# Normalization order, filler matmuls, V's bias and weight loads in the front of a fused attention and expert layer

## The reference, cut to what matters

```python
xn = _layernorm(x, axis=-1)
x = x + attn(xn) + ffn(xn)
# attn
q, k, v = proj(Wq, bq), proj(Wk, bk), proj(Wv, bv)
q, k = _apply_rope(q, sin, cos), _apply_rope(k, sin, cos)
attn = softmax(where(cam, q @ k.T * scale, neg))
out = (attn @ v) @ Wo.T + bo
# ffn
logits = xn @ router_w.T
top_vals, top_idx = top_k(logits, 2)
expert, weight = top_idx[:, 0], softmax(top_vals)[:, 0]
out = (silu(xn @ gate_w.T) * (xn @ up_w.T)) @ down_w.T   # of the row's expert
out = out * weight
```

## Time and profile before

| what | us |
|---|---|
| median of 3 runs | 379.81 |
| lowest and highest of them | 377.82, 380.61 |
| the profiled execution's own time | 378.44 |
| its span | 376.6 |
| TensorE busy | 360.9 |
| VectorE busy | 331.0 |
| ScalarE busy | 265.3 |
| GpSimd busy | 72.0 |

### The profile page before, as it was taken

One profiled execution on the slowest core, in us unless ns is written; L12 is line 12 of the kernel. 1 busy time (PEld: TensorE's weight loads), 2 busy tenths in 40 slices (PEclk: granted clock), 3 DMA queues, 4 the chain that ended last, 5 costly groups with the idle time before them and its releaser, 6 DMA issues.

```text
span 376.6 us, 12257 instructions
## 1 busy us (share of the span) xinstructions
PE 360.9 (96%) x4670; PEld 204.4 (54%) x4670; DVE 331.0 (88%) x684; ACT 265.3 (70%) x538; POOL 72.0 (19%) x87
## 2 busy tenths in 40 slices
PE   0899999999999999999999999999999999999996
PEld 0665467675664554555645555455455554643364
DVE  5779789997767999999999999999999999998655
ACT  1533567664445888888888888888888888899920
POOL 5001744553000020120210202121222020210002
PEclk9999999999999999999999999999999999999999
DMA  7999646765511212132232221232213222111116
GB/s 234 404 382 261 152 132 184 220 192 169 143 51 44 61 33 60 50 83 62 49 76 60 74 62 45 76 81 68 74 45 85 68 57 74 34 35 29 46 29 224
DMA packets 30794, 40.58 MB, mean 108 GB/s; under 512 B 10772, under 2 KB 25876, under 8 KB 30160
## 3 DMA queue, kind: packets, MB, share of 16 engines
q1 hardware_dynamic: 28680, 34.62, 30.8%
q0 software_dynamic: 1872, 5.11, 5.5%
q10 hardware_dynamic: 192, 0.13, 0.1%
HBM read 25.78 MB, written 11.70 MB: 100 GB/s over the span
## 4 chain that ended last, share of the span: by engine, by line
PE 92%; ACT 2%; DMA 2%; SPq 1%; issue 1%; DVE 1%; ACTq 0%; DVEq 0%
PE ps L791 22%; PE ps L821 21%; PE ps L716 14%; PE ps L667 7%; PE ps L729 6%; PE ps L594 5%; PE ps L680 5%; PE ps L799 3%; PE ps L705 2%; DMA bqk<-bqk_in 2%; PE ps L583 1%; PE ps L692 1%; PE ps L653 1%; PE ps L576 1%; PE ps L570 1%
## 5 line engine op out<-in xcount | busy, mean ns | idle before, releaser
L1125 DVE TENSOR_REDUCE mx<-ps 128x1 f32<-128x512 f32 x232 | 150.2, 683 | 3.7 <-PE ps L716 0.9
L1426 ACT ACTIVATE probs<-ps 128x512 f32<-128x512 f32 x192 | 101.8, 599 | 18.4 <-PE ps L821 17.4
L821 PE MATMUL ps<-q_op,k_op 98*32 98x512 bf16 (+1 forms) x1104 | 112.2, 381 | 0.2
L716 PE MATMUL ps<-k_op,q_op 96*32 96x512 bf16 x672 | 76.1, 381 | 0.0
L1128 DVE TENSOR_REDUCE mx_tail<-ps 128x2 f32<-128x410 f32 x116 | 66.8, 576 | 3.7 <-PE ps L729 3.5
L821 PEld LDWEIGHTS ps<-q_op,k_op 98*32 98x32 bf16 (+1 forms) x1104 | 39.3, 96 | 33.7 <-ACT wqk L1426 5.2
L791 PE MATMUL ps<-probs,v_op 128*32 128x512 f32 x384 | 52.5, 592 | 0.0
L502 POOL COPY v_op<-v_all 128x192 f32<-128x192 f32 x16 | 7.0, 443 | 187.5 <-PE ps L791 187.5
L1426 ACT ACTIVATE dn<-ps 77x512 f32<-77x512 f32 x64 | 34.2, 591 | 8.3 <-PE ps L821 8.2
L496 POOL DMA_INDIRECT o_st<-sorted_rows,token_of x23 | 28.2, 1228 | 57.0 <-DVE token_of L1054 29.2
L716 PEld LDWEIGHTS ps<-k_op,q_op 96*32 96x32 bf16 x672 | 25.1, 96 | 22.0 <-DVE mx L1125 9.6
(11 more groups left out here) (142 smaller groups left out, 490.1 us busy)
## 6 DMA issues: line engine op xcount, KB each, us to landing
q_parts<-parts SPq DMA_DIRECT2D x12, 256.0 KB, 2.8
sorted_results<-ys SPq DMA_DIRECT2D x23, 128.0 KB, 2.4
gu<-gu_in SPq DMA_DIRECT2D x1, 2816.0 KB, 11.5
q_op<-q_parts SPq DMA_DIRECT2D x11, 192.0 KB, 3.4
tab<-tab_in SPq DMA_DIRECT2D x1, 2048.0 KB, 11.3
sorted_rows<-xn SPq DMA_DIRECT2D x4, 512.0 KB, 5.9
xnT<-o_st SPq DMA_DIRECT2D x62, 32.0 KB, 2.3
tab<-softmax_recips SPq DMA_DIRECT2D x15, 128.0 KB
```

The lines of the kernel that those rows point to most:

```text
L716: ins = pe.matmul(bank(t % 2)[r:r + CW, :], q_op[slot][0:KR, P * t + r:P * t + r + CW], k_op[slot][0:KR, 0:NWIDE], start=True, stop=True)
L821: ins = pe.matmul(bank(4 + u % RING)[r:r + w, :], k_op[h % OPS][:, c0 + r:c0 + r + w], q_op[h % OPS][:, QB * b:QB * b + QB], start=True, s ...
L1125: dve.tensor_reduce(mx[:, slot, t:t + 1], bank(t % 2)[:, 0:NWIDE], AX.X, ALU.max).then_inc(wide_reduced, 1)
L1426: act.activation(prob[c][0:rows, QB * b:QB * b + QB], bank(4 + u % RING)[0:rows, :], ACT.Exp, scale=SCALE).then_inc(exp_done, 1)
```

## The change

- **Front, VectorE.** `moments` is split into `statistics` and `moments`. The order is now statistics, aggregates and normalization of a group, then the next group; the statistics of tiles 12 and 13 stand before the third normalization. The addition of the constant is gone: ScalarE's root takes it as its bias from a tile `eps`. The last group is normalized like the others, two tiles on each engine. VectorE copies the pair 6 to `xnT`, ScalarE the pair 7.
- **Front, ScalarE.** `root(g)` stands directly before the normalization of its own group, or a little before it. The bias of the first key half stands before the third normalization. ScalarE's queue issues the load of the identity matrix.
- **Front, TensorE.** VectorE writes zeros to a part of `q_op1`, and `keep_running` multiplies them, 512 columns at a time: 16 times at the start, and 6, 2, 2 and 2 times between the pairs. All logits are made in one group of eight matmuls. Two chunks of V stand before pairs 6 and 7, and half of projection 2 before the sums of the slots.
- **GpSimd** writes the ones of `v_all` first and those of the three `k_op` after the logits.
- **V's bias.** `add_bv` is gone. ScalarE copies V's chunks in its place (`copy_v`). Before head 0 TensorE multiplies bv, spread over the partitions, with wo, and VectorE adds the result to the output's bias, which is what GpSimd adds to x.
- **Loads.** x comes without other transfers between its groups. Keys' and queries' weights come separately, the tables in three parts. The middle part of the tables and `dn` are issued after a wait for the fourth gather, ahead of the remaining key parts; `wo` is issued at step 6.

The diff, cut:

```diff
@@ sync
-                if g == 1:
-                    sp.dma_start(const[:], const_d).then_inc(const_in, 16)
-                    sp.dma_start(rt[:], rt_d).then_inc(rt_in, 16)
...
+            load_tab(1)
             store_part(0, 0)
+            sp.wait_ge(xs_in[3], 16)
+            load_tab(2)
             sp.dma_start(dn[0:80, :], dn_d[0:80, :]).then_inc(down_in, 16)
             sp.dma_start(dn[80:IH, :], dn_d[80:IH, :]).then_inc(down_in, 16)
-            sp.wait_ge(xs_in[1], 16)
-            sp.dma_start(wo[:], wo_d).then_inc(wo_in, 16)
...
+                if s == 6:
+                    sp.dma_start(wo[:], wo_d).then_inc(wo_in, 16)
@@ tensor
+            def keep_running(times):
+                for _ in range(times):
+                    pe.matmul(bank(6), q_op[1][:, 0:P], q_op[1][:, 0:QB], start=True, stop=True)
+            pe.wait_ge(warm_ready, 1)
+            keep_running(16)
+            pe.wait_ge(ident_in, 16)
+            for pair in (0, 1):
+                turn_pair(pair)
+            keep_running(6)
+            for pair in (2, 3):
+                turn_pair(pair)
+            keep_running(2)
+            pe.wait_ge(wk_in, 16)
+            pe.wait_ge(xnT_ready, 1)
+            project(0)
...
+            project_v(V_ORDER[5])
+            pe.wait_ge(wq_in, 16)
+            project(2, (0,))
             pe.wait_ge(slot_ready, 1)
...
+            pe.wait_ge(wo_in, 16)
+            pe.wait_ge(bvo_in, 32)
+            for m in range(HC):
+                ins = pe.matmul(bank(3)[:, 0:HID], bv_col[:, m:m + 1].broadcast_to([P, P]),
+                                wo[:, HID * m:HID * m + HID], start=m == 0, stop=m == HC - 1)
+            ins.then_inc(bias_in_psum, 1)
             head_step(0, 0, first=True)
@@ vector
-                settle()
-                dve.tensor_scalar(var[:, 4 * g:4 * g + 4], mv[:, 4 * g:4 * g + 4, 1], EPS, None,
-                                  ALU.add).then_inc(var_ready, 1)
...
-            for g in range(1, 4):
-                moments(g)
-                normalize(g - 1)
+            statistics(0, 4)
+            moments(0)
+            normalize(0)
+            statistics(4, 8)
+            moments(1)
+            normalize(1)
+            statistics(8, 12)
+            moments(2)
+            statistics(12, 14)
+            normalize(2)
+            statistics(14, 16)
+            moments(3)
             normalize(3)
...
-            for n in range(NCH):
-                add_bv(n)
...
+            dve.wait_ge(bias_in_psum, 1)
+            dve.wait_ge(bvo_in, 32)
+            dve.tensor_tensor(bias, bank(3)[:, 0:HID], bias, ALU.add).then_inc(bias_ready, 1)
             head_step(0, 0, early=True)
@@ scalar
+            def copy_v(n):
+                c = V_ORDER[n]
+                rows = CHUNKS[c][1]
+                act.wait_ge(v_in_psum, n // 2 * 2 + 2)
+                act.copy(v_view[0:rows, :, c, 0:DH], v_bank(c).rearrange("p (h d) -> p h d", h=HEADS)
+                         ).then_inc(v_read, 1)
```

More of the change, by code:

```diff
@@ L115, in layer @@
         bvo = sb("bvo", [P, 2 * HID])
+        bias = bvo[:, HID:2 * HID]
+        bv_col = bvo[:, 0:HC]
         const = sb("const", [P, C_END])
@@ L211, in layer @@
         x_first = sem("x_first")
-        const_in, wqk_in, tab_in = sem("const_in"), sem("wqk_in"), sem("tab_in")
+        const_in, wk_in = sem("const_in"), sem("wk_in")
+        tab_in = [sem(f"tab_in{n}") for n in range(3)]
         wv_in, rt_in, gate_up_in, down_in, wo_in = (
             sem(n) for n in ("wv_in", "rt_in", "gate_up_in", "down_in", "wo_in"))
+        ident_in, wq_in, bqk_in, bvo_in = (sem(n) for n in ("ident_in", "wq_in", "bqk_in", "bvo_in"))
+        warm_ready = sem("warm_ready")
         dve_step = sem("dve_step")
@@ L479, in _ @@
         def _(pool):
-            for n in range(RING):
-                pool.memset(k_op[n][KR:KM, :], 1.0).then_inc(ones_ready, 1)
-                pool.wait_ge(ones_ready, n + 1)
+            pool.memset(v_all[:], 1.0).then_inc(ones_ready, 1)
+            pool.wait_ge(ones_ready, 1)
             pool.iota(lane, [[1, P]], base=0, channel_multiplier=0).then_inc(iota_ready, 1)
@@ L488, in _ @@
             pool.wait_ge(iota_ready, 3)
-            pool.memset(v_all[:], 1.0).then_inc(ones_ready, 1)
-            pool.wait_ge(ones_ready, RING + 1)
+            pool.wait_ge(logits_T_ready, 1)
+            for n in range(RING):
+                pool.memset(k_op[n][KR:KM, :], 1.0).then_inc(ones_ready, 1)
+                pool.wait_ge(ones_ready, n + 2)
             def gather(t):
@@ L533, in add_bias @@
             def add_bias(t):
-                pool.tensor_tensor(x_sb[:, t, :], x_sb[:, t, :], bvo[:, HID:2 * HID], ALU.add
+                if t == 0:
+                    pool.wait_ge(bias_ready, 1)
+                pool.tensor_tensor(x_sb[:, t, :], x_sb[:, t, :], bias, ALU.add
                                    ).then_inc(residual_ready, 1)
@@ L563, in turn_pair @@
                     pe.wait_ge(xnT_ready, pair - 3)
-                if pair % 2 == 0 or pair == NT // 2 - 1:
+                if pair % 2 == 0:
                     pe.wait_ge(xn_ready, pair // 2 + 1)
@@ L625, in _ @@
             ins.then_inc(logits_ready, 1)
-            for c in V_ORDER[2:4]:
+            for c in V_ORDER[3:5]:
                 project_v(c)
@@ L643, in _ @@
             ins.then_inc(slots_summed, 1)
-            for u in (2, 3):
-                project(u)
+            project(2, (1,))
+            project(3)
             def turn_rows(t):
@@ L897, in settle, with statistics @@
                 dve.wait_ge(dve_step, steps[0])
-            def moments(g):
-                for t in range(4 * g, 4 * g + 4):
+            def statistics(first, last):
+                for t in range(first, last):
                     if t == 0:
@@ L919, in normalize @@
                                          rstd[:, 4 * g:4 * g + 4], ALU.mult, ALU.mult).then_inc(scale_ready, 1)
-                for t in range(4 * g, 4 * g + (2 if g < 3 else 4)):
+                for t in range(4 * g, 4 * g + 2):
                     ins = dve.tensor_scalar(xn[:, t, :], x_sb[:, t, :], mv[:, t, 0:1], rstd[:, t:t + 1],
@@ L939, in _ @@
                                    0.0, None, ALU.is_gt))
+            dve.wait_ge(xT_in_psum, NT // 2 - 1)
+            dve.tensor_copy(xnT[:, :, S - 4 * P:S - 2 * P], bank(2).rearrange("p (m n) -> p m n", m=HC)
+                            ).then_inc(last_xnT_ready, 1)
             step(dve.tensor_scalar(same_token[:].rearrange("p (t e) -> p t e", t=NT),
@@ L1322, in biased @@
                                bias=bqk[:, col:col + 1], scale=1.0).then_inc(proj_read, 1)
+            act.dma_start(const[:, 0:C_TRI], const_d[:, 0:C_TRI]).then_inc(ident_in, 16)
             root(0)
-            for g in range(1, 4):
-                root(g)
-                normalize(g - 1)
-                copy_xT(2 * g - 2)
-                copy_xT(2 * g - 1)
-            copy_xT(6)
-            act.wait_ge(wqk_in, 32)
-            for odd in range(2):
-                biased(0, odd)
+            normalize(0)
+            copy_xT(0)
+            copy_xT(1)
+            root(1)
+            normalize(1)
+            copy_xT(2)
+            copy_xT(3)
+            root(2)
+            act.wait_ge(bqk_in, 16)
+            biased(0, 0)
+            normalize(2)
+            copy_xT(4)
+            root(3)
+            copy_xT(5)
+            normalize(3)
+            biased(0, 1)
+            copy_xT(7)
+            v_view = v_all[:].rearrange("p (h c w) -> p h c w", h=HEADS, c=NCH)
+            def copy_v(n):
[4 more added lines that the diff above has]
+                         ).then_inc(v_read, 1)
+            act.wait_ge(ones_ready, 1)
+            for n in (0, 1):
+                copy_v(n)
             act.wait_ge(logits_T_ready, 1)
@@ L1395, in _ @@
             highest(0)
+            for n in (2, 3):
+                copy_v(n)
             for odd in range(2):
                 biased(1, odd)
+            for n in (4, 5):
+                copy_v(n)
+            biased(2, 0)
             act.wait_ge(gap_ready, 1)
             act.activation(tk["ratio"][:], tk["gap"][:], ACT.Exp).then_inc(ratio_ready, 1)
-            for odd in range(2):
-                biased(2, odd)
+            biased(2, 1)
+            biased(3, 0)
             middle(0)
-            for odd in range(2):
-                biased(3, odd)
+            biased(3, 1)
             copy_rows(0)
```

87 lines of the change are left out of this document (40 added, 47 removed).

## The result

The changed kernel takes 385.57 us (median of 4 executions, 385.36 to 387.09) beside 379.96 for the kernel before, measured with it: ratio 1.0161, 95% interval 1.0124 to 1.0198. (The ratios in this document come with the measurements and are not quite the quotients of the medians, here 1.0148.) It is slower by 1.5 to 1.6%, where the forecast was 379.7 with a range up to 382.0. The profiled execution took 385.44 around a span of 383.5, which is 6.9 above the span of before (376.6).

The account below looks back on a forecast made before the run. TensorE, busy 96% of the span and carrying the chain of waits, was taken as the bound. Terms -0.8 + 0.7 = -0.1 on the median 379.81 gave 379.7 us; own range 378.5 to 380.7, eight in ten 375.6 to 382.0.

Parts of the forecast that it names:

- Part 1, the front: Reordered opening up to the first turn of gathered rows: TensorE gets there at 36.0 against 41.53, 5.5 us won if kept.
- rival C: Front zeros fail, TensorE stays at 1.2 GHz until 17, tokens no earlier than 34.8: +3.6, 383.4 us, chance 0.05.
- The stall of 0.8 us: VectorE's small operations in the opening: GpSimd lockout could return 0.8 us on the next one; none was counted.
- Part 2, the landing of the down weights: Down weights behind the fourth gather and tables' middle land at 51.6; TensorE stops 3.8 us before the first down product.
- rival B: TensorE's clock falls in the stop at the first down product: +1.0, with the bias +1.7, 381.5 us; chance 0.18.
- The cast: ScalarE's cast for projection 2 waits for stores behind the down weights until 52.4; VectorE's subtraction then wins nothing.
- Part 3, V's bias: Bias matmuls and VectorE's addition before head 0 delay its maxima: cost 0.4 to 1.2 us, taken as +0.7.
- TensorE's wait of 0.38: Before head 0, TensorE waited 0.38 us for ScalarE's last copy; the bias matmuls stand there, a maximum tile partly filling it.
- what part 1 leaves behind part 2: Front's gain remaining after the late down weights: taken as -0.8 us, bounds -5.5 to +1.
- rival A: Down weights load at 386 GB/s, not 217, and land at 48.7, nearly in time: -3.0, 376.8 us; chance 0.27.

Follow-up runs that it names:

- e6: Kernel before, with the down weights issued behind the fourth gather instead of behind the gate and up weights: 382.81 us, ratio 1.0092.
- e12: Changed kernel, with the stores of the other five key parts held back until the down weights have landed: 388.29 us, ratio 1.0232.
- e7: Changed kernel, with the first key group's two small parts stored ahead of SyncE's wait for the fourth gather: 385.47 us, ratio 1.0153.
- e1: Changed kernel without SyncE's wait for the fourth gather, order of transfers kept: 384.17 us, ratio 1.0153.
- e2: Changed kernel, wait kept, with the down weights issued ahead of the tables' middle: 384.05 us, ratio 1.0146.
- e4: Changed kernel, with V's bias added by VectorE as before and no product of bv and wo: 383.47 us, ratio 1.0115.
- e5: Changed kernel, down weights directly behind gate/up, then two small key parts, only the tables' middle behind the fourth gather: 378.62 us, ratio 0.998.
- e8: e5 with V's bias added on VectorE as before, without the bias product: 377.89 us, ratio 0.9949.
- e9: Changed kernel with the edits of e3 and e7 together: 383.56 us, ratio 1.0093.
- e3: Changed kernel, with 32 more zero matmuls on TensorE ahead of the wait for the down weights: 386.36 us, ratio 1.0207.
- e10: e8 with eight zero products ahead of the first turn of gathered rows: 377.61 us, ratio 0.9943.
- e11: e10 without the 28 zero products of the front: 378.08 us, ratio 0.9954.

## Why the prediction was wrong

**Part 1, the front, held.** First turned pair 7.77 (forecast 7.0), last copy of xnT ends at 18.8 (18.1), token numbers 31.66 (31.1), first turn of gathered rows 36.67 (36.0). The 0.7 us that is missing arises at the very start: the second half of the first group of x came 0.48 later than VectorE wanted it, and the small operations behind took the rest. The transposes run at full rate; rival C is out. The stall of 0.8 us that the prediction priced did not come back: VectorE's small operations in the first group took 0.38 (four aggregates), 0.18 and 0.16.

**Part 2, the landing of the down weights, is the step that failed.** The forecast put it at 51.6, with a stop of 3.8 us. It landed at 56.4, with a stop of 7.9. The 4.8 us between come from three terms:

- The wait ended at 40.66 instead of 40.1: +0.6.
- SyncE needs 0.57 and 0.60 us to issue the tables and the first part of the weights, so the last part is issued at 41.91. I had counted its issue at the wait's end: +1.25.
- The last part then took 14.47 us instead of 2.2 + 2.7 + 6.6 = 11.5: +3.0. In e6, with no tables ahead, it took 11.87, so the tables are worth about 2.6, as forecast (2.7), and the weights 11.87 - 2.2 = 9.7 instead of 6.6, or 149 GB/s and not 217.

Why 9.7 shows in the packet records of the traces, in which the weights have 88 packets of 16 KB. From the start of the first to the end of the last it takes 7.9 us in the kernel before (30.80 to 38.71), 9.1 in the changed kernel, 10.1 in e6 and 9.4 in e12. So the forecast was short by two things. First, I had read the rate in a stretch in the middle of the load: the same load took 7.9 us even in the trace of before, because its last eight packets need 1.7 us. Second, what else the DMA engines did in that time. The queue of GpSimd's gathers in it (packets, MB, share of 16 engines), in the order before (30.8 to 38.7), changed (46.1 to 55.2), e6 (42.8 to 53.0), e12 (47.0 to 56.4):

```profile
q0 software_dynamic: 41, 0.12, 7.8%
q0 software_dynamic: 135, 0.39, 23.8%
q0 software_dynamic: 110, 0.32, 25.2%
q0 software_dynamic: 139, 0.39, 25.4%
```

Before, the load ran nearly alone; behind the fourth gather it meets the gathers of the expert steps, and they take a quarter of the engines. The prediction says that gathers beside the load add, and adds nothing. By these shares they take 1.6 us (changed), 2.0 (e6) and 1.8 (e12) more of all 16 engines than before, and the load takes 1.2, 2.2 and 1.5 longer than before. So the sizes agree, but no run kept the gathers away from the load.

**The clock was rival B, and belonged in the sum.** I gave it 0.18 and 1 us. It fell in the stops of 7.9 us and more of the changed kernel, e7 and e12, and in those of e1, e2, e4, e5, e6 and e8, which were 1.9 to 5.7 us long. The Trainium skill, page "TensorE: Matmul & The Clock Gate", Part 1, was cited for it in the prediction; the trace agrees with it, and the 0.96 and 0.50 of the windows are the row. I had weighed the rule and left it out of the sum, and it was one side of the tie that e9 measured at 2.0 to 2.6 us.

**The cast.** The forecast had it start at 52.4, held by the stores behind the weights. The mechanism is as described, it started at 58.00 since the weights were late. But I let the cast decide alone. e7 takes it away and gains nothing, e3 takes the fall of the clock away and gains nothing, both together give 2.0 to 2.6.

**Part 3, V's bias, held.** Forecast +0.7, bounds 0.4 to 1.2; measured 1.0 over fourteen profiles. The length of the product was right (0.88 in the chain, 0.87 forecast). What I had set against it, TensorE's wait of 0.38, was not there to fill.

**The sum.** Forecast -0.8 + 0.7 = -0.1. The spans say +5.6 at the last down product, and +1.3 behind it. The forecast's bound for what part 1 leaves behind part 2 ended at +1, because I took the clock and the landing as separate mishaps; a late landing brings the stop, the slow clock and the late stores all at once. A slowdown of more than 1% had got a chance of 0.05.

**What settles it.** e6 makes more than half of the loss by moving the load in the kernel before (+3.8 us by the medians beside it, 3.5 by the ratio), e5 undoes it all by moving the load back in the changed kernel (ratio 0.998); that e5 also stores two key parts earlier is not what does it, since by itself that gained nothing (e7). The 6.9 us of the spans are of both signs: the front wins 4.5 us up to the first down product, the late weights lose 7.9 in the stop and 2.2 behind it, and 1.3 go behind the last down product, 1.0 of them to the bias product. With the weights in their old place and without the product it is 0.5% faster (e8, e10). Why the lead of the front is then worth 2 us at most is partly shown: the first gather now runs beside the weights, lands 6.2 us behind its issue instead of 3.4 (e5), and the clock falls in the stop.

## What to carry to other kernels

Time a load that gates something from its own issue to its landing, in the profile, and not by the rate of its middle; ask what else will use the DMA engines at its new place, and count each instruction that the issuing queue has ahead of it. When a front gets faster, ask first what is now needed earlier, and load that before anything else. A stop of TensorE costs its length and then the slow clock behind it, unless something fills it; and where two edits each give nothing, try them together before calling both harmless.

## What the runs showed of the hardware that was not expected

- The down weights, 88 rows of 16 KB, took 9.7 us beyond the fixed part in e6 (149 GB/s), and the DMA share stood at 0.9 or above for most of it, while at 10 to 12 us 386 GB/s moved at a share of 1.05.
- Packets of the same 16 KB differ by what they carry: the 128 of the tables took 0.61 us each in the kernel before (27 GB/s on one engine), the 88 of the down weights 1.15 us there and 1.13 to 1.16 in the changed kernel, e6 and e12 (14 GB/s). Sixteen engines at that pace make 229 GB/s, near the 217 that rival A put down to the moment; in four traces it is the pace of this load wherever it stands. What makes its packets slow no run shows.
- An indirect gather beside a bulk load landed after 6.2 us (e5) or 9.3 us (e1), instead of 3.4.
- TensorE's granted clock went from 1.00 to 0.50 around an idle time of 2.3 us (e5), and in the changed kernel within one of 7.9. In e8, an idle time of 1.90 us was followed by a projection of 2.66 us in place of 1.88.
- The granted clock is printed as 1.00 in the opening of the kernel before and of e11, while the durations there (1.94 us for eight turned pieces, 1.06 in the changed kernel once the zeros have run) are those of 1.2 GHz.
